# Norms of two token chunks moved from the router stage into the attention stage

## The reference, cut to what matters

```
x = x + layernorm(attention(layernorm(x)))        # 16 heads of 16, causal, ALiBi
x = x + layernorm(moe(layernorm(x)))              # what follows is moe
  logits = flat @ router_w;  scores = softmax(logits)
  topk_idx = top 4 of (logits + router_bias)      # of 64 experts
  routed = sum over the 4 of score * (silu(x wg) * (x wu)) wd
  shared = sum of 2 shared experts, (silu(x swg) * (x swu)) swd, for every token
  return routed + shared
```

## Time and profile before

| | us |
|---|---|
| median of 3 runs | 1357.13 (1357.02 to 1359.3) |
| profiled execution, device time | 1368.52 |
| its span | 1366.7 |
| TensorE busy in the span | 1165.0 (85%) |
| VectorE busy | 856.2 (63%) |
| ScalarE busy | 621.4 (45%) |
| GpSimd busy | 356.2 (26%) |

### The profile page before, as it was taken

How to read it: one execution, slowest core, us unless ns; L and a number is a source line. 1 busy time by engine, 2 the same in 40 slices (tenths; PEclk the granted TensorE clock), 3 DMA queues, 4 the chain that set the end, 5 groups by cost and what they waited for, 6 DMA issues and landing times. The chain is left out here.

```text
span 1366.7 us, 25308 instructions
## 1 busy us (share of the span) xinstructions
PE 1165.0 (85%) x9088; PEld 972.4 (71%) x9088; DVE 856.2 (63%) x2160; ACT 621.4 (45%) x1420; POOL 356.2 (26%) x458
## 2 busy tenths in 40 slices
PE   6669996666399987767779999999999999999895
PEld 5536774555298976545648888888888888888775
DVE  6458884885356655677455666656656666664474
ACT  5425442602134442357634554554455545553664
POOL 3321110266601436573034005001500140000110
PEclk9879998558699998777799999999999999999998
DMA  6725766122399763254243323223342342221001
GB/s 174 177 74 151 239 197 256 54 77 85 113 361 395 279 248 117 85 161 139 83 119 101 85 94 121 82 80 101 115 145 79 101 117 78 80 92 67 1 17 47
DMA packets 77961, 177.21 MB, mean 130 GB/s; under 512 B 12614, under 2 KB 26182, under 8 KB 75270
## 3 DMA queue, kind: packets, MB, share of 16 engines
q1 hardware_dynamic: 71564, 158.54, 35.6%
q0 software_dynamic: 6272, 17.05, 4.0%
HBM read 114.26 MB, written 61.08 MB: 128 GB/s over the span
## 5 line engine op out<-in xcount | busy, mean ns | idle before, releaser
L2258 ACT ACTIVATE decay<-masked,negcum 128x128 f32<-128x128 f32 x512 | 164.0, 391 | 240.8 <-issue 156.2
L2174 PE MATMUL joint<-xh,w_high 128*128 128x512 f32 x512 | 211.7, 413 | 1.1 <-POOL wl L2115 1.1
L2174 PE MATMUL joint<-xh,wl 128*128 128x512 f32 x512 | 200.6, 392 | 0.0
L2174 PE MATMUL joint<-xl,w_high 128*128 128x512 f32 x512 | 199.7, 390 | 0.0
L2363 DVE COPY cT<-joint 128x512 f32<-128x512 f32 x128 | 88.3, 690 | 177.6 <-PE joint L2174 177.6
L2185 PEld LDWEIGHTS pcb<-cT,bT 128*128 128x128 f32 x1024 | 134.5, 191 | 10.6
L2185 PE MATMUL pcb<-cT,bT 128*128 128x128 f32 x1024 | 135.3, 275 | 0.0
L2112 POOL TENSOR_TENSOR w_high<-w_in,none 128x512 fp32r<-128x512 f32 x32 | 34.7, 1086 | 319.5 <-DMA w_in<-in_w_bc 226.1
L2174 PEld LDWEIGHTS joint<-xh,w_high 128*128 128x128 f32 x512 | 96.5, 188 | 21.9 <-issue 4.8
L2174 PEld LDWEIGHTS joint<-xh,wl 128*128 128x128 f32 x512 | 96.1, 188 | 21.1
L2174 PEld LDWEIGHTS joint<-xl,w_high 128*128 128x128 f32 x512 | 96.6, 189 | 15.3
(11 more groups left out here) (381 smaller groups left out, 2716.4 us busy)
## 6 DMA issues: line engine op xcount, KB each, us to landing
cumrow<-ssm_cum SPq DMA_DIRECT2D x128, 256.0 KB, 3.3
slots_in<-blank SPq DMA_DIRECT2D x16, 1024.0 KB, 5.7
xg<-slots_in SPq DMA_DIRECT2D x32, 512.0 KB, 5.4
slots_out<-spare SPq DMA_DIRECT2D x32, 512.0 KB, 3.9
weights<-in_expert_quads SPq DMA_DIRECT2D x16, 768.0 KB, 9.0
w_in<-in_w_bc SPq DMA_DIRECT2D x32, 256.0 KB, 3.7
qk_parts<-parts SPq DMA_DIRECT2D x32, 192.0 KB, 2.5
stack<-qk_parts SPq DMA_DIRECT2D x32, 192.0 KB, 3.3
```

The costliest lines, as they stand in the source:

```text
L2174: last = nc.tensor.matmul(bank[:], w[:, j, col:col + P], a[:, k, c * CHUNK:(c + 1) * CHUNK], start=(m == 0), stop=(m == len(parts) - 1))
L2258: last = nc.scalar.activation(decay[:, n % 2, o], masked[:, n % 2, o], ACT.Exp, bias=negcum[:, c * TPC + i, head:head + 1])
```

## The change

In `stage_attention` the norm of y, the addition to x and the norm of x into `rows` are done for chunks 0 and 1. `block_norms` puts VectorE's share at the second step of a block, behind `normalise`: y statistics of two tiles in blocks 5, 7, 9, 11; measures of y in 8 and 12; x statistics in 10 and 14; measures of x in 12 and 16. ScalarE scales y in blocks 9 and 13 and writes the rows in blocks 13 and 17. GpSimd does `spread` and the addition x + y, behind its splits. `stage_route` then keeps only chunks 2 and 3; the deviations of x for these stand on GpSimd between the sixth and the seventh scatter, and the orders on TensorE, ScalarE and VectorE are changed.

The raw weights get a place each: where the low halves lie. All five loads are issued first in attention; the high parts follow at steps -6 to -2, the low parts (in place) in blocks 14 to 18. The fills are one per unit from unit 0, behind `place`.

`rows` and the norms' tiles are now allocated ahead of attention; the later buffers of gathered rows are views of `rows`.

```diff
+FIRST_HIGH, FIRST_LOW = 2 - HALF, 14
+EARLY_NORMS = 2
+Y_STATS, Y_MEASURE, X_STATS, X_MEASURE = 5, 8, 10, 12
+Y_SCALE, ROWS = 9, 13
+def chunk_at(block, first):
+    g, at = divmod(block - first, 4)
+    return g if at == 0 and 0 <= g < EARLY_NORMS else None
-FILLS = {u: 1 for u in range(4, UNITS - 2)}
-FILLS.update({UNITS - 2: 3, UNITS - 1: 3})
...
 # attention, SP
+                for r in range(RAWS):
+                    load_raw(r)
                 for u in range(LEAD):
                     place(u)
...
                 for u in range(UNITS):
                     if u + FIRST_UNITS < UNITS:
                         load(u + FIRST_UNITS)
-                    if u < RAWS:
-                        load_raw(u)
-                    for _ in range(FILLS.get(u, 0)):
-                        if filled == 0:
-                            sp.wait_ge(blank_set, 1)
-                        fill(sp, blank, filled)
-                        filled += 1
                     if u + LEAD < UNITS:
                         place(u + LEAD)
+                    if u == 0:
+                        sp.wait_ge(blank_set, 1)
+                    fill(sp, blank, u)
 # attention, GpSimd
+                for u in range(UNITS + 2):
+                    if u < UNITS:
+                        split(u)
+                    g = chunk_at(u, Y_MEASURE + 1)
+                    if g is not None:
+                        pool.wait_ge(y_measured, g + 1)
+                        spread(nc, norm_step, norms, OF_Y, tiles(g)).then_inc(y_spread, 1)
+                    g = chunk_at(u, Y_SCALE + 1)
+                    if g is not None:
+                        part = slice(g * TPC, (g + 1) * TPC)
+                        pool.wait_ge(y_scaled, g + 1)
+                        nc.gpsimd.tensor_tensor(flat(x[:, part, :]), flat(x[:, part, :]), flat(y[:, part, :]),
+                                                ALU.add).then_inc(x_added, 1)
+                    g = chunk_at(u, X_MEASURE + 1)
+                    if g is not None:
+                        pool.wait_ge(x_measured, g + 1)
+                        spread(nc, norm_step, norms, OF_X, tiles(g)).then_inc(x_spread, 1)
 # attention, ScalarE
-                for i in range(-LEAD * HALF, STEPS + HALF):
+                for i in range(-LEAD * HALF, STEPS + 2 * HALF):
...
-                    if i % HALF == AT_BLOCK and FIRST_RAW <= i // HALF < FIRST_RAW + RAWS:
-                        high(i // HALF - FIRST_RAW)
+                    g = chunk_at(i // HALF, Y_SCALE) if i % HALF == AT_BLOCK else None
+                    if g is not None:
+                        act.wait_ge(y_spread, g + 1)
+                        for m in tiles(g):
+                            last = normal(nc, norms, y[:, m, :], y[:, m, :], OF_Y, m)
+                        last.then_inc(y_scaled, 1)
+                    g = chunk_at(i // HALF, ROWS) if i % HALF == AT_BLOCK else None
+                    if g is not None:
+                        act.wait_ge(x_spread, g + 1)
+                        for m in tiles(g):
+                            normal(nc, norms, rows[:, m, :], x[:, m, :], OF_X, m)
+                    if FIRST_HIGH <= i < FIRST_HIGH + RAWS:
+                        high(i - FIRST_HIGH)
 # attention, VectorE
+                def block_norms(at):
+                    seq = (at - Y_STATS) // 2
+                    if (at - Y_STATS) % 2 == 0 and 0 <= seq < 2 * EARLY_NORMS:
+                        dve.wait_ge(y_ready, seq + 1)
+                        for m in (2 * seq, 2 * seq + 1):
+                            last = nc.vector.bn_stats(norms["stats"][:, OF_Y, m, :], y[:, m, :])
+                        link(last)
+                    g = chunk_at(at, Y_MEASURE)
+                    if g is not None:
+                        measure(nc, link, norms, OF_Y, tiles(g)).then_inc(y_measured, 1)
+                    g = chunk_at(at, X_STATS)
+                    if g is not None:
+                        dve.wait_ge(x_added, g + 1)
+                        for m in tiles(g):
+                            last = nc.vector.bn_stats(norms["stats"][:, OF_X, m, :], x[:, m, :])
+                        link(last)
+                    g = chunk_at(at, X_MEASURE)
+                    if g is not None:
+                        measure(nc, link, norms, OF_X, tiles(g)).then_inc(x_measured, 1)
...
-                    if i % HALF == AT_BLOCK + 1 and FIRST_RAW <= i // HALF < FIRST_RAW + RAWS:
-                        low(i // HALF - FIRST_RAW)
+                        block_norms(u + 2)
+                    if i % HALF == AT_BLOCK + 1 and FIRST_LOW <= i // HALF < FIRST_LOW + RAWS:
+                        low(i // HALF - FIRST_LOW)
 # route, GpSimd
+                for g in range(EARLY_NORMS, NCH):
+                    deviations(OF_Y, g)
...
                             n = i * TOPK + k
+                            if n == BEFORE_ROWS:                  # 6
+                                for late in range(EARLY_NORMS, NCH):
+                                    deviations(OF_X, late)
 # route, TensorE
                 turn(1)
                 score(0)
                 score(1)
-                turn(2)
                 place_chunk(0)
                 place_chunk(1)
+                turn(2)
+                score(2)
                 turn(3)
-                score(2)
                 score(3)
 # route, ScalarE
-                scale_y(0)
-                scale_y(1)
-                fill_rows(0)
                 high_parts(0)
-                fill_rows(1)
+                high_parts(1)
                 scale_y(2)
-                high_parts(1)
                 scale_y(3)
                 fill_rows(2)
 # route, VectorE, the order after the change
+   statistics(y, OF_Y, 2); memsets; set_tables(); low_parts(0); low_parts(1); statistics(y, OF_Y, 3)
+   choose(0); add(2); choose(1); tables(0); find_slots(0)
+   statistics(x, OF_X, 2); add(3); statistics(x, OF_X, 3); find_slots(1)
+   low_parts(2); choose(2); low_parts(3); choose(3); tables(1); find_slots(2)   # then as before
```

More of the change, by code:

```diff
@@ L455, in load_stack, with stage_attention @@
                          src.rearrange("r (c j) l -> (r c) (j l)", c=HD)).then_inc(in_loaded[u % ROOM], 16)
-FILLS = {u: 1 for u in range(4, UNITS - 2)}
-FILLS.update({UNITS - 2: 3, UNITS - 1: 3})
-def stage_attention(chip, vpad, qk_dram, stack, consts, router, y, ident, blank, fill, xs_clear, ins):
+def stage_attention(chip, x, vpad, qk_dram, stack, consts, router, y, rows, norms, ident, blank, fill, xs_clear, ins):
     nc = chip.nc
@@ L559, in _, with split @@
                 link = linker(pool, split_link)
-                for u in range(UNITS):
+                norm_step = linker(pool, norm_link)
+                norm_step(nc.gpsimd.memset(norms["power"][:], -0.5))
+                def split(u):
                     pool.wait_ge(shift_out, u + 1)
@@ L764, with stage_moe @@
 I32 = mybir.dt.int32
-def stage_moe(chip, begun, router, spare, x, xh, xl, y, ident, xs, ys, t, ins):
+def stage_moe(chip, begun, router, spare, x, rows, norms, xh, xl, y, ident, xs, ys, t, ins):
     with ExitStack() as same:
[L769 to L772, removed]
+        ahead = {"weights": chip.memory(same)[0]("weights", [P, NE, WEXP])}
+    ahead["xg"] = rows[:, 0:DEEP * QUAD, :].rearrange("p (n s) d -> p n s d", s=QUAD)
+    ahead["rest"] = flat(rows[:, DEEP * QUAD:, :])
     ahead["x_loaded"] = [chip.kept_sem("x_loaded") for _ in range(DEEP)]
@@ L775, in stage_moe @@
     with ExitStack() as room:
[L776 to L779, removed]
+        chip.memory(room)[0]("held", [P, AHEAD * QUAD, WEXP])
+        stage_route(chip, x, rows, norms, xh, xl, y, ident, xs, t, ahead, router, ins)
     begun.close()
     with ExitStack() as room:
-        sb, _ = chip.memory(room)
-        sb("taken", [P, NT * D + NE * WEXP])
+        chip.memory(room)[0]("taken", [P, NE, WEXP])
         stage_slots(chip, spare, ident, xs, ys, ahead, t, ins)
@@ L796, in load_experts, with stage_route @@
     sp.dma_start(ahead["weights"][:, q * QUAD:(q + 1) * QUAD, :], ins["expert_quads"][q, :, :, :]).then_inc(done, 16)
-def stage_route(chip, x, rows, xh, xl, y, ident, xs, t, ahead, router, ins):
+def stage_route(chip, x, rows, norms, xh, xl, y, ident, xs, t, ahead, router, ins):
     nc = chip.nc
@@ L829, in stage_route @@
         until = sb("until", [P, PARTIES, NE])
-        norms = {name: sb("norm_" + name, [P, NORMS, NT] + tail)
-                 for name, tail in (("stats", [6]), ("moments", [2]), ("negmean", []), ("var", []), ("rstd", []),
-                                    ("shift", []))}
-        norms["power"] = sb("power", [P, TPC])
         before = sb("before", [P, PARTIES, NE])
@@ L884, in _, with deviations @@
                 link = linker(pool, pool_link)
-                link(nc.gpsimd.memset(norms["power"][:], -0.5))
-                for kind, g in NORM_ORDER:
+                def deviations(kind, g):
                     pool.wait_ge(var_ready, normed(kind, g))
```

(5 more changed lines are left out.)

70 lines of the change are left out of this document (40 added, 30 removed).

## The result

The changed kernel takes 1347.78 us (median, 1347.03 to 1348.19) against 1358.22 (1357.02 to 1361.72) for the kernel before on the same chip: ratio 0.992, 95% interval 0.9893 to 0.9948. Two more comparisons on other chips gave 0.9891 (0.987 to 0.9912) and 0.9898 (0.9866 to 0.993). So it is about 1% faster, 10 to 17 us by the medians, and the forecast of 14 lies within that. The profiled execution took 1348.19 us, span 1346.4.

A forecast was written before the change was run, and what follows sets the result against it. Bounds: VectorE in attention's odd blocks, a chain over all engines, then GpSimd's scatter. Slots stage 12.3 us sooner, with attention 14.5, taken as 14.2: 1357.1 - 14.2 = 1342.9, say 1343; likeliest case 1339 to 1348 (chance 0.62), overall 1337 to 1354.

The forecast's parts named there:

- Shared experts level with the scatter: End of the route stage: scatter would allow the slots stage at 363.8, shared experts at 363.9, their 15 us slack used up.
- Attention: Attention as a whole: -6.0 + 2.8 + 1.0 = -2.2 us, between -7 and +11 with the bounds.
- Raws: Raw weights loaded first in attention, low parts moved to late blocks: attention 6.0 us shorter, bounds 3.8 to 7.5.
- Fills: Attention, one 1 MB fill per unit from unit 0, behind the shift rows: costs 0.
- rival D: Attention's odd blocks: fills hold up the shift rows, 3.6 us in each of eight, 29 us, total 1372; chance 0.08.
- Odd-block statistics: Blocks 5, 7, 9 and 11: two tiles of y statistics each on VectorE, no gap to hide in, 2.8 us longer.
- Block 13: Attention's block 13: ScalarE gets two jobs, 4.2 us against 2.87 idle; 1.0 us longer taken.
- Even blocks: Blocks 8 to 16, even: VectorE's 0.7 or 1.4 us of norm work each stays hidden in its 2.2 us gap.
- rival B: Attention pays for the norms it hosts: +7.6 us there, net gain 4.7, total 1352 (1349 to 1354); chance 0.17.
- Route head: From attention's last addition to the first scatter: 28.9 us in place of 43.9.
- Scatter: The 64 scatters take 92.6 us as before, plus 2.6 for two deviations after the sixth; no starving for chunk 2.
- Rival C: Shared experts set the stage's end, their unnamed waits double: 12 us more leaves 1355, 5 us leaves 1348; chance 0.07.

The follow-up runs named there:

- raws_only: The kernel before with only the raw weights' early loads and late low parts added: 1355.62 us, ratio 0.9942 to the kernel before.
- even_stats: The changed kernel with y statistics one block later, in even blocks 6, 8, 10 and 12: 1340.47 us, ratio 0.9888 to the kernel before.
- rows12: The changed kernel with the two late deviations behind the twelfth scatter instead of the sixth: 1348.48 us, ratio 0.9905 to the kernel before.
- fills_late: The changed kernel with fills back at units 4 to 13 and three each in the last two: 1342.55 us, ratio 0.989 to the kernel before.
- combo_again: The changed kernel with late fills, y statistics in even blocks and chunk 0's rows in block 14, repeated: 1346.03 us, ratio 0.9853.
- flight4_again: The changed kernel with four scatters in flight instead of two, repeated on another chip: 1359.7 us, ratio 0.998 to the kernel before.
- combo: The changed kernel with late fills, y statistics in even blocks and chunk 0's rows in block 14: 1342.44 us, ratio 0.9861.
- before_again: The kernel before, unchanged, timed and profiled again: 1356.74 us, ratio 1.0003.
- after_again: The changed kernel, unchanged, timed and profiled again: 1342.43 us, ratio 0.9891 to the kernel before.
- after_third: The changed kernel, unchanged, on the chip of combo_again and combo_early: 1348.89 us, ratio 0.9898 to the kernel before.
- combo_early: The changed kernel with y statistics in even blocks and chunk 0's rows in block 14, fills from unit 0: 1350.43 us, ratio 0.9887.

## Why the prediction was right

The forecast was 1343 us and 1347.78 was measured, 4.8 more and just inside the likeliest case's 1339 to 1348. Of the 4.8, 1.1 is the kernel before, slower here than the 1357.13 that I started from; the rest is a difference of 10.4 in place of 14.2. The main mechanism held: the scatter starts sooner and the stage ends by it. Luck helped in two places: attention's errors cancel, and the wrong term for the shared experts stood no higher than the scatter's.

**Attention, -2.2 forecast, -2.4 measured: right by errors that cancel.** The spacings of the reciprocals split it: up to block 2, -4.7; blocks 2 to 6, 0.0; 6 to 13, +1.4; 13 to 17, +0.9; the tail -0.1.
- Raws: forecast -6.0, bounds 3.8 to 7.5, measured -8.7 in raws_only. I counted half of ScalarE's 5.09 us in block 1, and took part of the blocks' 5.0 for a lower clock that stays. The first came back nearly whole (4.3 us up to block 2), and of the second 4.1. The lower clock did not stay (1.00 in raws_only where before has 0.50). The term was mis-sized.
- Fills: forecast 0, measured +3.6 in blocks 2 to 4, up to 4.8 of attention in all. I looked for them at the shift rows in the odd blocks; they struck the stack rows in the first units. It is rival D's mechanism at an eighth of its price. The Trainium skill (DMA: Bandwidth & Descriptors, Queues, rings and completion order) says that one ring's descriptors are consumed in its order; the load behind the fill, with the 1.65 us wait, agrees. My sign for this rival, a wait for shift rows, could not tell: within attention TensorE waited for them 3.5 us in all before the change and 2.4 after it.
- Odd-block statistics: forecast 4 x 0.70 = 2.8. One spacing went from 6.80 to 7.37, 4 x 0.57 = 2.3, and even_stats took it back.
- Block 13: forecast +1.0; its spacing went from 5.69 to 6.46, +0.8, and the next from 5.90 to 6.07. With chunk 0's rows in block 14 it is 5.69 and 5.90 again.
- Even blocks: forecast hidden. VectorE's gap fell from 2.20 to 1.23 (at 194.45), and the four even spacings went from 9.21, 9.47, 9.47 and 9.47 to 9.22, 9.22, 9.30 and 9.62. Right but for the last, 0.15 longer. So rival B is out.
- GpSimd's addition took 2.36 us (2.2 forecast), and no spacing shows it. VectorE's maxima beside it, one input in PSUM, kept their 0.42 us. The Trainium skill (SBUF — State Buffer, Who interferes with whom) says such a pair does not meet; the trace agrees. GpSimd's own rows in block 9:

```profile
167.66 2.36 POOL L591 TENSOR_TENSOR x<-x,y 128x1024 f32<-128x1024 f32 x1 [0.36 <-ACT y L452]
```

The upper bound of +11 for attention was a slip: with all 17 us exposed and the lower bound of 3.8 for the raws it is +13. Nothing hangs on it.

**Route head, 28.9 forecast, 26.7 measured** (25.7 to 27.3 in nine executions of the changed kernel and its variants, 28.5 to 28.6 in five). The steps from the tables on fit: 250.59 to 260.10 is 9.5, as forecast. All 2.2 us are gained before them, by the clock: I priced the score matmuls at the 0.21 us a piece of the earlier trace rows, all at the clock's lower level. The changed kernel's windows of 2 us and, behind them, those of rows12, which has the same instructions up to there:

```profile
236.00:238.00 2.00, 0.68 (x7) 0.69 (x7) 1.87 (x7) 0.00 (x0) 1.11 (x2) 1.00 0.96 383
238.00:240.00 2.00, 2.00 (x18) 2.00 (x17) 1.82 (x5) 1.99 (x5) 0.00 (x0) 0.84 1.02 421
240.00:242.00 2.00, 2.00 (x12) 2.00 (x11) 1.68 (x9) 0.57 (x2) 0.59 (x1) 0.50 1.04 433
```

```profile
236.00:238.00 2.00, 2.00 (x12) 2.00 (x11) 1.36 (x4) 1.33 (x3) 0.00 (x0) 0.50 1.00 415
238.00:240.00 2.00, 2.00 (x11) 2.00 (x11) 1.93 (x10) 1.23 (x3) 0.00 (x0) 0.50 1.01 424
```

At the upper level (1.00 is 2.4 GHz) the first scores follow each other every 0.11 us, at 0.50 every 0.21. Where the clock stayed at 0.50 throughout the head (fills_late, rows12, combo_again, flight4_again) the head took 28.53 to 28.56: the forecast's own case, 0.3 to 0.4 off. What decides between the two is not shown. It is not how long attention took: at 153.1 (rows12) the head was long, and at 147.5 (combo) short.

**Scatter: +2.6 forecast, in its place.** The sixth ends at 268.07, the seventh starts at 270.83. It never starves. The whole is 4.05 longer (95.73 against 91.68), 3.95 in the repeated pair (93.95 against 90.0), 2.0 in the second traces (94.28 against 92.28). The difference to the forecast's 2.6 is not established, since the same 64 scatters without the deviations took 90.0 to 93.4 in four executions.

**Shared experts level with the scatter: wrong, and harmless by luck.** I moved the profiled execution's end (360.6) by 3.0. But that execution held 17.9 us of unnamed waits there (11.3 + 6.6, on two engines and partly side by side), and the repetition without them ended 11.4 sooner. In the changed kernel these experts ended at 350.8, so TensorE's pause before the slots stage was 12.69 us where I had said under 3. The sum escaped since the scatter's term, 363.8, stood as high as theirs, 363.9. Rival C got its 0.07 from the same reading. Its waits are real and need some 11 us before they count; with two scatters in flight they did so in 2 of the 12 executions of the changed kernel and its variants.

**Sum.** The slots stage starts 13.9, 15.7 and 17.3 us sooner in the three pairs, 14.5 forecast, and 14.2 was taken. (The first has 1.6 us against it that arise before attention's first maxima.) The medians give 10.4, 14.3 and 16.6 on three chips. In the end a sum for the start of one stage was the right quantity. The difference of two profiled spans, 20.3, would have misled.

## What to carry to other kernels

Read a stage's slack from more than one execution, or take out the waits that name no work: here they made a chain of 349 us look like one of 361. Host moved work in the blocks where the bounding engine has a gap (even blocks: free; odd blocks: 0.57 us for 0.70 us of work), and keep large transfers out of the queue as long as the pipeline is still filling, even if the steady blocks do not mind them (here 3.6 us of attention). The stage behind can differ by some us between executions of the same instructions, by its clock or by unnamed waits, so look for a gain at a fixed later point too, and in more than one execution.

## What the runs showed that I had not expected

- TensorE's granted clock where the route stage starts differs between executions of the same instructions (from 236 to 238 us 1.00 in the changed kernel's first profile, 0.50 in rows12), for 1.3 to 2.9 us of route head.
- Behind a wait of 1.65 us in the first blocks the granted clock went from 1.00 to 0.50, and two blocks took 3.6 us longer, the wait included.
- Four indirect transfers in flight made the issue even (1.27 us), and another engine's instruction wait 18.6 and 19.3 us with no named cause.
- Waits without a named cause come and go with two scatters in flight as well. Within a stage they reach from none (before_again, after_again) to 12 us on ScalarE's line in the second layer (before, after_third) and 16.7 and 18.8 us on VectorE's line in the shared experts (combo_early, second trace of even_stats).
